# Softmax sums of sixteen heads in one tile: one reciprocal and two shuffles in place of two reciprocals

## The chip, the cores and the metric

The kernel runs on one core of a Trainium2 chip. The metric is the device time of one execution in microseconds (us), taken as the median of several runs. The core's engines are TensorE (PE in the profile, its weight loads PEld), VectorE (DVE), ScalarE (ACT), GpSimd (POOL) and SyncE (SP, which issues transfers). PSUM is the memory that TensorE writes, in banks of 512 f32 columns by 128 partitions.

## The reference

Two layers over x of shape (2, 1024, 256) and a context of shape (2, 64, 192), cut to what matters here:

```python
# layer 0: cross attention with 16 heads of 16 columns, 64 keys, then a small MLP
q = (x @ Wq + bq).reshape(B, N, 16, 16)
k = (y @ Wk + bk).reshape(B, M, 16, 16)
v = (y @ Wv + bv).reshape(B, M, 16, 16)
attn = softmax(einsum('bnhd,bmhd->bhnm', q, k) * scale)
out = einsum('bhnm,bmhd->bnhd', attn, v).reshape(B, N, 256)
x = x + (relu(out @ W1 + b1) @ W2 + b2)      # q is computed from layernorm(x)
# then: a gated LoRA FFN with 8 experts (wi, wo, lora_A, lora_B, gate_w), top 2,
# layer 1: single-head cross attention, and a linear layer with pooled columns
```

The change touches the division by the sums of the first softmax.

## The kernel before, in words

The 2048 rows are worked in 8 blocks of T = 256 rows. Three stages are in flight at once: `body(a, f, c, h)` runs, on each engine, the first attention and MLP of block a, the FFN of block f = a - 1, the last attention of block c = a - 2, and the queries of block h = a + 1. Below, "block a" means the pass whose first attention is block a. Passes 0 and 1 have no c and take the `else` branches; passes 2 to 7 take the `if C_` branches. After the passes come `drain` and `end`. Each engine has its own program written out by hand, in a fixed order; engines meet only at semaphores, and an engine that waits holds everything behind it in its own order.

Products that need more than fp32r precision are made as three passes over high and low halves (`passes`, L341, and `three`, L332): high by high, low by high, high by low. The high half comes from ACT, the low half from POOL or DVE.

Attention of a block on PE: `a_scores(a, d)` (L411) makes scores of four heads for d = 0 to 3 into `psS`; ACT's `exps` (L896) turns them into `ex`, where a chunk c of 8 holds a pair of heads, 64 keys each, on 128 partitions. `a_attend(a, m)` (m = 0, 1) then takes four chunks. For each it multiplies the values (L425) into 32 partitions of bank `P_(m)`, columns 0 to 255, and a matrix of ones, `ones_pair`, into columns 256 to 511 of the same rows (L426), so each head's sum stands on the 16 partitions of that head. After each m it signals `pv`.

DVE's `attended(a, m)` waits for `pv`, takes the reciprocal of the 128x256 sums (L1193, to `rec`), waits for it, and multiplies the values by it into `o32` (L1195). ACT's `attended` makes the high half `oa_h` (L901), POOL's `attended_low` the low half `oa_l` (L1562). PE's `a_hidden(a, 0)` (L341, `psS<-oa_h,w_h`) waits for both high halves, and before its third pass for both low halves.

Around it, in the order of each engine:

- PE in pass 0: scores 2, two filler products, attend 0, scores 3, attend 1, `values1` (L608), transposes (L356), fillers, `a_hidden(0, 0)`. In pass 1: attend 0, second products of FFN parts 0 and 1 (L490), scores 3, `f_base` 2 (L332), attend 1, `f_first` 2, `f_base` 3, `f_second` 2, `f_first` 3, `a_hidden(1, 0)`, transposes that wait for `gw`, `a_hidden(1, 1)`, `a_queries` (whose third pass waits for `xta_l`). In passes 2 to 7: attend 0, attend 1, `f_second` 1, `c_transpose` (L547), `f_base` 2, `f_first` 2, `c_attend` (L557, waits for `et_l`), `f_base` 3 (waits for the sum of FFN part 1), and so on to `a_hidden`.
- DVE in passes 2 to 7: `hidden_sum` 0 (L1252), `attended` 0, `hidden_sum` 1, `weights_low` (L1282, makes `et_l`), `attended` 1, then the sums and residuals of block c. In passes 0 and 1: `hidden_sum` 0 and 1 (pass 1 only), `attended` 0, `attended` 1, and in pass 1 then `gw` (L1411), `hidden_sum` 2, `vv_l` (L1417), `xta_l` (L1163).
- ACT in pass 0 after its two `attended`: `xta_h` (L863), then the high halves of the weights w2 and wi (L965, `w_h` and `wi_h`), then `hidden` (L907) and what follows it. `first_relu` 2 is L927.

The ones come with the load `kept` of 424 columns (32 + 256 + 8 + 128), issued third on the SP queue.

Of the kernel before, what the change touches and what calls it, by code (L numbers as in the profile page):

```python
# [11 lines left out]
P = 128  # L12
BATCH, SEQ, D = 2, 1024, 256
KEYS, DC = 64, 192
# [36 lines left out]


FIRST = [("ident", P), ("cols", 20), ("kmask", 8), ("pmask", 2)]
KEPT = [("ones_pair", PW), ("b2row", D), ("gbrow", EXPERTS), ("eid", P)]

VROWS = [("vmask", D), ("bvrow0", D)]
PASSING = [("bvrow1", D), ("wq1t", KC * D)]
# [3 lines left out]
def build(nc, io):  # L61
# [8 lines left out]
    def r3(t, a, lo=0, hi=None, rows=P):  # L70

        v = t[0:rows, lo:hi] if hi is not None else t[0:rows, lo:]
        return v.rearrange("p (a n) -> p a n", a=a)
# [40 lines left out]
    def views(t, parts):  # L114
        out, at = {}, 0
        for n, width in parts:
            out[n] = t[:, at:at + width]
            at += width
        return out
# [1 line left out]
    first = sb("first", [P, sum(n for _, n in FIRST)])  # L121
    kept = sb("kept", [P, sum(n for _, n in KEPT)])
    ident, cols, kmask, pmask = (views(first, FIRST)[n] for n, _ in FIRST)
    ones_pair, b2row, gbrow, eid = (views(kept, KEPT)[n] for n, _ in KEPT)
    nbi = sb("nbi", [P, NFF])
    crow = sb("crow", [P, D])
    mhalf = sb("mhalf", [P, NT])
# [44 lines left out]
    EX = r3(ex, PAIRS)  # L172
    rec, o32 = sb("rec", [P, KC * T]), sb("o32", [P, KC * T])
    REC, O32 = r3(rec, KC), r3(o32, KC)
    lnst = {j: (sb(f"st{j}", [P, NT * 6]), sb(f"mv{j}", [P, NT * 2]), sb(f"ve{j}", [P, NT]), sb(f"nm{j}", [P, NT]),
                sb(f"rs{j}", [P, NT]), sb(f"nmr{j}", [P, NT])) for j in (1, 2, 3, 4)}
    lg, srt, srtd, srte = (sb(n, [P, NT * EXPERTS]) for n in ("lg", "srt", "srtd", "srte"))
# [47 lines left out]
    with block:  # L225
# [97 lines left out]
        def _(pe):  # L323
# [91 lines left out]
            def a_attend(b, m):  # L415

                if m == 0 and b % BPB == 0:
                    pe.wait_ge(S("v0_ready"), b // BPB + 1)
                    pe.wait_ge(S("ld_kept"), 16)
                at = b // BPB * D  # L420
                for d in (2 * m, 2 * m + 1):
                    pe.wait_ge(S("ex"), b * DPAIRS + d + 1)
                    for c in (2 * d, 2 * d + 1):
                        rows = slice(PW * (c % GPC), PW * (c % GPC) + PW)
                        mm(P_(m)[rows, 0:T], v0[:, at + c * PW:at + (c + 1) * PW], EX[:, c, :], start=True, stop=True)  # L425
                        last = mm(P_(m)[rows, T:2 * T], ones_pair, EX[:, c, :], start=True, stop=True)  # L426
                last.then_inc(S("pv"), 1)

            def a_hidden(b, u):
                if u == 0:  # L430
# [421 lines left out]
        def _(act):  # L852
# [46 lines left out]
            def attended(b, m):  # L899
                act.wait_ge(S("o32"), b * KC + m + 1)  # L900
                A(OA[0][:, m, :], O32[:, m, :], ACT.Identity).then_inc(S("oh"), 1)  # L901
# [20 lines left out]
            def first_relu(b, u, bank=None):  # L922
                bank = I_(u % 2) if bank is None else bank
                act.wait_ge(S("first_ps"), b * NDF + u + 1)
                for k in range(2):
                    f = 2 * u + k
                    last = A(R1[:, f, :], bank[:, k * T:(k + 1) * T], ACT.Relu, bias=cols[:, BI + f:BI + f + 1])  # L927
                last.then_inc(S("r1"), 1)
# [82 lines left out]
            def body(a, f, c, h):  # L1011
                A_, F_, C_, H_ = (v is not None for v in (a, f, c, h))
                if A_:
                    exps(a, 0)
                if F_:
                    lora_high(f)
                if A_:
                    exps(a, 1)
                if f == 0:
                    act.wait_ge(S("v1t_ps"), 1)  # L1020
                    A(v1t[:, :], T_(0), ACT.Identity).then_inc(S("v1t"), 1)
                    act.wait_ge(S("v1"), 1)
                    A(VV[0][:, 0:2 * BATCH:2, :], r3(v1, BATCH), ACT.Identity).then_inc(S("vv_h"), 1)
                if C_:
                    linear(c)
                    first_relu(f, 0)
                    exps(a, 2)
                    exps(a, 3)
                    weights_exp(c)
                    first_relu(f, 1)  # L1030
                    if H_ and h < TURNED:
                        normalise(1, h, XIN)
                    elif H_:
                        across_high(h)
                    sum_high(f, 0)
                    weights_high(c)
                    attended(a, 0)
                    sum_high(f, 1)
                    first_relu(f, 2)
                else:  # L1040
                    if F_:
                        first_relu(f, 0)
                        first_relu(f, 1)
                    exps(a, 2)
                    if F_:
                        sum_high(f, 0)
                    exps(a, 3)
                    normalise(1, h, XIN)
                    if F_:
                        sum_high(f, 1)  # L1050
                    attended(a, 0)
                    if F_:
                        first_relu(f, 2)
                if A_:
                    attended(a, 1)
                if F_:
                    first_relu(f, 3)
                if f == 0:
                    act.wait_ge(S("gw"), 1)
                    A(gw_h[:, :], gw[:, :], ACT.Identity).then_inc(S("gw_h"), 1)  # L1060
                if a == 0:
                    high(1, h, XTA, T_(1))
                    high_weights("w2")
                    high_weights("wi")
                if f == 0:
                    high(1, h, XTA, T_(1))
                if A_:
                    hidden(a, 0)
                    hidden_high(a, 0)
                    hidden(a, 1)  # L1070
                if C_:
                    hidden_high(a, 1)
                if H_:
                    queries(h)
                if A_ and not C_:
                    hidden_high(a, 1)
                if a == TURNED - 2:
                    centred_high()
                if f == 0:
                    act.wait_ge(S("vw_ps"), 1)  # L1080
                    A(VV[0][:, 1:2 * BATCH:2, :], T_(0).rearrange("p (b n) -> p b n", b=BATCH), ACT.Identity).then_inc(
                        S("vv_h"), 1)
                if a == 0:
                    high_weights("ga")
                    high_weights("lb")
                    high_weights("wo")
                if F_:
                    sum_high(f, 2)
                    sum_high(f, 3)
                if A_:  # L1090
                    normalise(2, a, XMID)
                    high(2, a, XTF, T_(1))
                if a == 0:
                    act.wait_ge(S("g_ps"), 1)
                    for b in range(BATCH):
                        A(GWR[:, :, b * (KEYS + D):b * (KEYS + D) + KEYS],
                          T_(0)[:, 0:KC * P].rearrange("p (c b k) -> p c b k", c=KC, b=BATCH)[:, :, b, :],
                          ACT.Identity).then_inc(S("g_in"), 1)
                    act.wait_ge(S("gb_ps"), 1)
                    A(gb[:, :], I_(0)[:, 0:P], ACT.Identity).then_inc(S("gb"), 1)  # L1100
                if H_:
                    maxima(h)
                if F_:
                    high(3, f, XTC, T_(0))
                if A_:
                    sorted_exps(a)
                if C_:
                    store(c)
# [29 lines left out]
        def _(dve):  # L1138
# [48 lines left out]
            def row_max(b, t, ps=psS):  # L1187
                dve.wait_ge(S("row_sc"), b * NT + t + 1)
                V.reduce_max(MX[:, t, :], ps[:, :].rearrange("p (h k) -> p h k", h=HEADS), AX.X).then_inc(S("mx"), 1)

            def attended(b, m):
                dve.wait_ge(S("pv"), b * KC + m + 1)
                V.reciprocal(REC[:, m, :], P_(m)[:, T:2 * T]).then_inc(S("rec"), 1)  # L1193
                dve.wait_ge(S("rec"), b * KC + m + 1)
                V.tensor_tensor(O32[:, m, :], P_(m)[:, 0:T], REC[:, m, :], MULT).then_inc(S("o32"), 1)  # L1195

            def first_residual(b):
# [187 lines left out]
            def body(a, f, c, h):  # L1385
# [7 lines left out]
                    norm_stats(1, h, XIN)  # L1393
                if C_:
                    hidden_sum(f, 0)
                    attended(a, 0)
                    hidden_sum(f, 1)
                    weights_low(c)
                    attended(a, 1)
                    weights_sums(c)  # L1400
                    third_residual(c)
                    scaled_linear(c)
                else:
                    if F_:
                        hidden_sum(f, 0)
                        hidden_sum(f, 1)
                    attended(a, 0)
                    attended(a, 1)
                if f == 0:
# [359 lines left out]
```

## Time and profile before

| | |
|---|---|
| median of 3 runs | 321.26 us (321.03 to 321.32) |
| span of the profiled execution | 319.5 us, first to last instruction |
| time of the profiled execution itself | not given apart; the median less the span is 1.8 us |
| mean granted TensorE clock | 0.989 of full speed |
| PE busy | 307.6 us, 96% |
| DVE busy | 233.1 us, 73% |
| ACT busy | 170.4 us, 53% |
| POOL busy | 161.4 us, 51% |

Busy shares are averages over stages with different limits. The span starts with loads and the first block, when weights are still being split into halves; it ends with a drain in which less and less work is left. The time of a change is read from the place where it lengthens or shortens what is waited for last.

### The profile page before, as it was taken

The page shows a single profiled execution, that of the slowest core. Times are in us where ns is not written, and L with a number is a line of the kernel's source. Part 1 is how long each engine was busy: PE and PEld are TensorE (multiplying, and loading weights), DVE is VectorE, ACT ScalarE, POOL GpSimd, SP SyncE. Part 2 cuts the span into 40 slices and gives each one's busy share as a digit, 9 for nine tenths or more (in the row PEclk, how much of TensorE's full clock was granted, in tenths as well). Part 3 has the DMA queues.
Part 4 walks back from the last instruction along what each step waited for, and adds up shares of the span by engine and source line. Part 5 has one row for each costly group of instructions (what it writes and reads, how often), then busy time and mean ns, then how long its engine had stood idle before and what let it go on. Part 6 is the DMA issues. An engine that isn't in the chain of part 4 may idle for free.

```text
span 319.5 us, 6462 instructions
## 1 busy us (share of the span) xinstructions
PE 307.6 (96%) x2469; PEld 281.6 (88%) x2469; DVE 233.1 (73%) x648; ACT 170.4 (53%) x346; POOL 161.4 (51%) x155
## 2 busy tenths in 40 slices
PE   7889999999999999999999999999999999999973
PEld 5658897899989998999989998999899989999961
DVE  4766775967986977867896689678868779456665
ACT  3447755682575358455647457635753574434520
POOL 2574683695055704672286407560557143703561
PEclk9999999999999999999999999999999999999995
DMA  7479730013101240114020421033022200000000
GB/s 254 141 240 383 195 84 2 0 31 78 60 1 19 69 131 0 18 41 125 35 19 17 92 92 16 3 91 109 1 18 64 69 4 0 2 25 10 0 33 33
DMA packets 16861, 20.80 MB, mean 65 GB/s; under 512 B 3104, under 2 KB 12832, under 8 KB 16576
## 3 DMA queue, kind: packets, MB, share of 16 engines
q1 hardware_dynamic: 14800, 16.97, 20.0%
q10 hardware_dynamic: 2032, 3.44, 3.1%
q8 instruction: 19, 0.31, 0.4%
q14 instruction: 10, 0.08, 0.1%
HBM read 11.48 MB, written 2.63 MB: 44 GB/s over the span
## 4 chain that ended last, share of the span: by engine, by line
PE 82%; DVE 6%; ACT 5%; DMA 2%; POOL 2%; SPq 2%; issue 1%; DVEq 0%; POOLq 0%
PE psI L332 14%; PE psI L490 14%; PE psP L341 11%; PE psI L341 10%; PE psS L341 6%; PE psT L332 4%; PE psP L425 3%; PE psS L411 2%; PE psP L426 2%; PE psT L557 2%; PE psT L356 2%; PE psS L388 2%; PE psP L654 1%; DMA xin<-in_x 1%; PE psS L332 1%; PE psP L466 1%
## 5 line engine op out<-in xcount | busy, mean ns | idle before, releaser
L1554 POOL TENSOR_TENSOR rs<-ve,mhalf 128x2 f32<-128x2 f32 x30 | 22.5, 749 | 96.8 <-DVE ve L1159 96.8
L1573 POOL TENSOR_TENSOR hid_l<-r,hid_h 128x512 fp32r<-128x512 f32 x32 | 42.2, 1330 | 16.8 <-ACT hid_h L932 16.6
L927 ACT ACTIVATE r<-psI,first 128x256 f32<-128x256 f32 x60 | 25.2, 477 | 19.8 <-PE psI L490 19.8
L490 PE MATMUL psI<-at_h,lb_h 128*128 128x256 f32 x120 | 35.1, 292 | 0.0
L1252 DVE SCALAR_TENSOR_TENSOR r<-psI,nbi,r 128x256 f32<-128x256 f32 x60 | 26.1, 477 | 11.4 <-PE psI L490 11.4
L490 PE MATMUL psI<-at_l,lb_h 128*128 128x256 f32 x120 | 33.9, 282 | 0.0
L490 PE MATMUL psI<-at_h,lb_l 128*128 128x256 f32 x120 | 33.7, 281 | 0.0
L1567 POOL TENSOR_TENSOR hs_l<-hs,hs_h 128x512 fp32r<-128x512 f32 x16 | 20.9, 1307 | 21.8 <-ACT hs_h L912 21.0
L1193 DVE RECIPROCAL rec<-psP 128x256 f32<-128x256 f32 x16 | 28.0, 1753 | 2.7 <-PE psP L426 2.7
L858 ACT ACTIVATE xn<-xmid,nmr,rs 128x256 f32<-128x256 f32 x16 | 8.8, 594 | 38.0 <-POOL nmr L1558 38.0
L896 ACT ACTIVATE ex<-psS 128x512 f32<-128x512 f32 x32 | 18.3, 599 | 19.0 <-PE psS L411 18.9
L490 PEld LDWEIGHTS psI<-at_h,lb_h 128*128 128x128 f32 x120 | 22.6, 188 | 3.9 <-issue 3.5
L332 PE MATMUL psI<-xtf_h,wi_h 128*128 128x256 f32 x120 | 25.9, 297 | 0.0
L332 PE MATMUL psI<-xtf_h,wi_l 128*128 128x256 f32 x120 | 24.1, 282 | 0.0
L332 PE MATMUL psI<-xtf_l,wi_h 128*128 128x256 f32 x120 | 23.9, 280 | 0.0
L932 ACT ACTIVATE hid_h<-r 128x512 fp32r<-128x512 f32 x32 | 19.6, 630 | 6.0 <-DVE r L1252 6.0
L490 PEld LDWEIGHTS psI<-at_h,lb_l 128*128 128x128 f32 x120 | 22.6, 189 | 0.0
L490 PEld LDWEIGHTS psI<-at_l,lb_h 128*128 128x128 f32 x120 | 22.6, 188 | 0.0
L332 PEld LDWEIGHTS psI<-xtf_h,wi_h 128*128 128x128 f32 x120 | 18.2, 189 | 2.4 <-issue 2.2
L890 ACT ACTIVATE stack<-psP 16x1024 fp32r<-16x1024 f32 x16 | 16.2, 1015 | 4.4 <-PE psP L397 4.1
L332 PEld LDWEIGHTS psI<-xtf_l,wi_h 128*128 128x128 f32 x120 | 18.4, 188 | 0.0
L332 PEld LDWEIGHTS psI<-xtf_h,wi_l 128*128 128x128 f32 x120 | 18.4, 188 | 0.0
(274 smaller groups left out, 868.2 us busy)
## 6 DMA issues: line engine op xcount, KB each, us to landing
stack<-qu_h SPq DMA_DIRECT2D x60, 64.0 KB, 2.0
xin<-in_x SPq DMA_DIRECT2D x8, 256.0 KB, 2.9
stack<-qu_l SPq DMA_DIRECT2D x30, 64.0 KB, 2.0
out<-x ACTq DMA_DIRECT2D x7, 256.0 KB, 2.0
xn<-in_xt SPq DMA_DIRECT2D x5, 256.0 KB, 3.0
raw_wi<-in_wi SPq DMA_DIRECT2D x1, 1024.0 KB, 7.9
raw_wo<-in_wo SPq DMA_DIRECT2D x1, 1024.0 KB, 10.3
kv<-in_kv SPq DMA_DIRECT2D x2, 384.0 KB, 5.2
```

Source lines behind the costliest of these rows:

```text
L332: last = mm(out, lhs(a, c), rhs(b, c), start=start and q == 0 and k == 0, stop=stop and q == 2 and k == n - 1, **kw)
L341: last = mm(out, lhs(a, c), rhs(b, c), start=start and (a, b) == pairs[0] and i == 0 and k == 0, stop=stop and k == len(chunks) - 1, skip_ ...
L490: last = mm(bank[:, k * T:(k + 1) * T], (WH, WL)[x]["lb"][:, 0, f * P:(f + 1) * P], AT[y][:, which, :], start=False, stop=q == 2, skip_gro ...
L890: A(QS[3 * PW:SROWS, :, t * P:(t + 1) * P], P_(1)[t * MXW:t * MXW + HEADS, 0:P].unsqueeze(1).broadcast_to([HEADS, PAIRS, P]), ACT.Identity ...
L896: A(EX[:, 2 * d:2 * d + 2, :], S_(d % 2).rearrange("p (k n) -> p k n", k=2), ACT.Exp, scale=SCALE).then_inc(S("ex"), 1)
L927: last = A(R1[:, f, :], bank[:, k * T:(k + 1) * T], ACT.Relu, bias=cols[:, BI + f:BI + f + 1])
L932: A(HH[:, 2 * u:2 * u + 2, :], R1[:, 2 * u:2 * u + 2, :], ACT.Identity).then_inc(S("hidh"), 1)
L1193: V.reciprocal(REC[:, m, :], P_(m)[:, T:2 * T]).then_inc(S("rec"), 1)
L1252: last = V.scalar_tensor_tensor(out=R1[:, f, :], in0=bank[:, k * T:(k + 1) * T], scalar=nbi[:, f:f + 1], in1=R1[:, f, :], op0=MAX, op1=ADD)
L1554: G_.tensor_tensor(rs[:, :], ve[:, :], mhalf[:, :], ALU.pow).then_inc(S(f"ln{j}_rs"), 1)
L1567: G_.tensor_tensor(HS[1][:, two, :], HS32[:, two, :], as32(HS[0][:, two, :]), ALU.subtract).then_inc(S("hsl"), 1)
L1573: G_.tensor_tensor(HL[:, two, :], R1[:, two, :], as32(HH[:, two, :]), ALU.subtract).then_inc(S("hidl"), 1)
```

## The change

The ones become `ones_lanes`, two 128x32 matrices. Matrix m sends a pair's two sums to 8 partitions each of its 32: the first head to partitions 8m to 8m + 7, the second to 16 + 8m to 16 + 8m + 7, and zeros to the others. The products with both matrices are accumulated in one tile, columns 256 to 511 of bank `P_(1)`, which after both halves of `a_attend` holds the sums of all 16 heads on 8 partitions each. `pv` is signalled once a block instead of twice. DVE takes one reciprocal of that tile (`inverses`), and `attended(a, m)` spreads it over the 16 partitions of each head with a `stream_shuffle` within groups of 32 partitions, then multiplies as before. In passes 2 to 7 `inverses` stands where `attended` 0 stood, and `attended` 0 moves behind `weights_low`. On ACT, `attended` 0 moves behind `first_relu` 2. The number of matrix products stays the same. `kept` grows by 32 columns.

```diff
-KEPT = [("ones_pair", PW), ("b2row", D), ("gbrow", EXPERTS), ("eid", P)]
+LANES = 8
+KEPT = [("ones_lanes", KC * PW), ("b2row", D), ("gbrow", EXPERTS), ("eid", P)]
...
+    INV = REC[:, 1, :]
...
-                        mm(P_(m)[rows, 0:T], v0[:, at + c * PW:at + (c + 1) * PW], EX[:, c, :], start=True, stop=True)
-                        last = mm(P_(m)[rows, T:2 * T], ones_pair, EX[:, c, :], start=True, stop=True)
-                last.then_inc(S("pv"), 1)
+                        mm(P_(m)[rows, 0:T], v0[:, at + c * PW:at + (c + 1) * PW], EX[:, c, :], start=m == 0, stop=True,
+                           skip_group_check=True)
+                        last = mm(P_(1)[rows, T:2 * T], ones_lanes[:, m * PW:(m + 1) * PW], EX[:, c, :], start=m == 0,
+                                  stop=m == 1, skip_group_check=True)
+                if m == 1:
+                    last.then_inc(S("pv"), 1)
...
(ACT, both branches of body)
-                    attended(a, 0)
                     sum_high(f, 1)
                     first_relu(f, 2)
+                    attended(a, 0)
...
(DVE)
+            def inverses(b):
+                dve.wait_ge(S("pv"), b + 1)
+                V.reciprocal(INV, P_(1)[:, T:2 * T]).then_inc(S("rec"), 1)
+
             def attended(b, m):
-                dve.wait_ge(S("pv"), b * KC + m + 1)
-                V.reciprocal(REC[:, m, :], P_(m)[:, T:2 * T]).then_inc(S("rec"), 1)
-                dve.wait_ge(S("rec"), b * KC + m + 1)
+                if m == 0:
+                    dve.wait_ge(S("rec"), b * 3 + 1)
+                even, odd = LANES * m, HD + LANES * m
+                V.stream_shuffle(REC[:, m, :], INV, [even] * HD + [odd] * HD).then_inc(S("rec"), 1)
+                dve.wait_ge(S("rec"), b * 3 + 2 + m)
                 V.tensor_tensor(O32[:, m, :], P_(m)[:, 0:T], REC[:, m, :], MULT).then_inc(S("o32"), 1)
...
                     hidden_sum(f, 0)
-                    attended(a, 0)
+                    inverses(a)
                     hidden_sum(f, 1)
                     weights_low(c)
+                    attended(a, 0)
                     attended(a, 1)
...
                         hidden_sum(f, 1)
+                    inverses(a)
                     attended(a, 0)
                     attended(a, 1)
```

## Rows read from the trace of the kernel before

**Rows 1.** Part 1 of the page: busy time, share of the span, instructions.
```profile
PE 307.6 (96%) x2469; PEld 281.6 (88%) x2469; DVE 233.1 (73%) x648; ACT 170.4 (53%) x346; POOL 161.4 (51%) x155
```

**Rows 2.** Busy time by stretch: start:end, length, engines, granted clock, DMA share, GB/s.
```profile
10.00:20.00 10.00, 8.79 (x45) 6.66 (x44) 8.99 (x15) 4.03 (x6) 6.94 (x4) 1.00 0.55 150
29.00:37.00 8.00, 7.84 (x61) 7.20 (x60) 4.32 (x5) 7.97 (x13) 5.96 (x5) 1.00 0.93 312
82.00:116.00 34.00, 34.00 (x293) 32.21 (x292) 26.27 (x78) 19.27 (x40) 17.12 (x17) 1.00 0.19 42
...
310.00:314.00 4.00, 2.69 (x9) 1.61 (x8) 2.56 (x11) 1.40 (x5) 0.22 (x1) 0.81 0.00 0
```

**Rows 3.** Waits of PE from 60 to 290 us: total, times, longest.
```profile
PE psT L356 <- ACT xn L858: 0.3, 1, 0.3
PE psP L341 <- POOL hs_l L1567: 0.2, 1, 0.2
```

**Rows 4.** Chain that ended last, in pass 0: start, us, what.
```profile
25.78 1.69 DVE rec L1193
...
27.95 0.42 ACT oa_h L901
...
28.86 0.95 ACT w_h L965
29.80 1.80 ACT wi_h L965
...
35.07 1.30 POOL hs_l L1567
...
36.41 1.22 PE psP L341 x8
```

**Rows 5.** Groups of DVE instructions: busy, mean ns of one, idle before.
```profile
L1193 DVE RECIPROCAL rec<-psP 128x256 f32<-128x256 f32 x16 | 28.0, 1753 | 2.7 <-PE psP L426 2.7
...
L1163 DVE TENSOR_TENSOR xtf_l<-psT,xtf_h 128x512 fp32r<-128x512 f32 x8 | 5.5, 692 | 12.9 <-ACT xtf_h L863 12.9
...
L1219 DVE MATCH_VALUE_LOAD idx<-srt,lg 128x8 f32 x16 | 1.3, 79 | 0.0
...
L1536 DVE COPY wqm<-psI 128x256 f32<-128x256 f32 x1 | 0.4, 425 | 0.1
...
L1509 DVE MEMSET zeros<- 128x256 f32 x1 | 0.3, 272 | 0.0
```

**Rows 6.** Timeline of pass 0: start, us, instruction, idle before.
```profile
25.36 0.42 DVE L1195 TENSOR_TENSOR o<-psP,rec 128x256 f32<-128x256 f32 x1
25.70 1.76 DVE L1193 RECIPROCAL rec<-psP 128x256 f32<-128x256 f32 x1
...
27.49 0.42 DVE L1195 TENSOR_TENSOR o<-psP,rec 128x256 f32<-128x256 f32 x1
```

**Rows 7.** Timeline of pass 1.
```profile
61.49 0.42 ACT L901 ACTIVATE oa_h<-o 128x256 fp32r<-128x256 f32 x1 [0.56 <-DVE o L1195]
...
62.74 0.64 PE L341 MATMUL psS<-oa_h,w_h 128*128 128x256 f32 x4
...
65.55 0.68 DVE L1163 TENSOR_TENSOR xta_l<-psT,xta_h 128x512 fp32r<-128x512 f32 x1
...
66.98 0.64 PE L341 MATMUL psP<-xta_l,wq_h 128*128 128x256 f32 x4
```

**Rows 8.** Timeline of pass 2.
```profile
90.54 0.66 PE L425 MATMUL psP<-ex,v 128*32 128x256 f32 x8
...
91.86 0.65 PE L426 MATMUL psP<-ex,kept 128*32 128x256 f32 x8
...
93.86 0.86 DVE L1252 SCALAR_TENSOR_TENSOR r<-psI,nbi,r 128x256 f32<-128x256 f32 x2
...
94.64 0.28 DVE L1282 TENSOR_TENSOR et_l<-psT,et_h 128x128 fp32r<-128x128 f32 x1
...
95.59 0.50 PE L557 MATMUL psT<-vv_h,et_h 64*128 64x512 f32 x2
```

More of the change, by code:

```diff
@@ L123, in build @@
     ident, cols, kmask, pmask = (views(first, FIRST)[n] for n, _ in FIRST)
-    ones_pair, b2row, gbrow, eid = (views(kept, KEPT)[n] for n, _ in KEPT)
+    ones_lanes, b2row, gbrow, eid = (views(kept, KEPT)[n] for n, _ in KEPT)
     nbi = sb("nbi", [P, NFF])
@@ L1395, in body @@
                     hidden_sum(f, 0)
-                    attended(a, 0)
+                    inverses(a)
                     hidden_sum(f, 1)
                     weights_low(c)
+                    attended(a, 0)
                     attended(a, 1)
@@ L1731 @@
         "vmask": (p[:, None] // KEYS == (c[None, :] // HD) % 2).astype(np.float32),
-        "ones_pair": (p[:, None] // KEYS == np.arange(PW)[None, :] // HD).astype(np.float32),
+        "ones_lanes": (2 * (p[:, None] // KEYS) + np.arange(KC * PW)[None, :] // PW
+                       == np.arange(KC * PW)[None, :] % PW // LANES).astype(np.float32),
         "eid": np.broadcast_to((p // RANK).astype(np.float32)[None, :], (P, P)),
```

## The prediction

> **What bounds the kernel now.** I read four views in this order. The page's busy times come first: PE works 96% of the span [rows 1], so time taken from DVE is worth something only where PE, or whoever holds PE up, waits for DVE. The second view is the busy time by stretch, which says where PE is not full. In a whole pass of the steady part it is busy 34.00 of 34.00 us, while DVE works 26.27 of them [rows 2]. The third is the list of PE's waits: from 60 to 290 us they come to 0.5 us, none of them for DVE [rows 3]. So the six passes 2 to 7 have no idle PE time that a lighter DVE could win back. The fourth is the chain that ended last. It is PE nearly everywhere from 36.41 us on, but in pass 0 it runs through the very instructions that are changed: the reciprocal, the multiply, `oa_h` on ACT, then without a gap `xta_h`, `w_h`, `wi_h`, `hidden` and what follows, POOL's `hs_l`, and PE at 36.41 [rows 4]. PE itself is busy 7.84 of 8 us there [rows 2], partly with fillers, and yet the chain is ACT's: whatever makes `oa_h` of m = 1 later moves the end of the kernel one for one. The question is thus not what DVE saves, but how long the road is from the last attention product to the second `oa_h`.
>
> **What the change removes and adds on DVE.** Gone in each block is one reciprocal of 1.753 us [rows 5]. Two shuffles of 128x256 are added. The trace has no shuffle. The nearest rows are the copy of 128x256, 0.425 us, and below it the memset of the same size, 0.272 us, which reads nothing; above, the 128x512 subtraction, 0.692 us, twice the columns [rows 5]. A shuffle is a copy through a permutation, with as many columns as the copy, so I take 0.42 us, and keep 0.27 and 0.69 for the range. The Trainium skill (VectorE: DVE Perf Modes, "The perf-mode tier table (the rule you actually need)") gives a shuffle about 2400 ns at 2048 columns. My estimate from that page is 0.30 us for 256, which would make the sum below 0.5 us smaller; no row here shows a shuffle.
>
> A shuffle also needs its permutation. The nearest row for handing an engine such a small table is `MATCH_VALUE_LOAD`, 0.079 us ahead of each index search [rows 5]. I take 0.08 us ahead of each shuffle, with 0 and 0.16 as bounds. The Trainium skill (Vector Engine (DVE) Microarchitecture Reference, section 3.8) has the selection written by an instruction of its own before the shuffle, and gives no time for it.
>
> DVE's work falls by 1.753 - 2 x (0.42 + 0.08) = 0.75 us a block, 6 us in all. Off the path, this is worth nothing.
>
> **The road in pass 0.** Before, the first reciprocal and multiply run while PE still does attend 1, and the second reciprocal starts at 25.70; its multiply starts at 27.49 and ends at 27.91 [rows 6]. An instruction that waits for its forerunner thus starts 0.03 us after that one's end, and one that needs nothing of it starts 0.34 us after the start of a multiply (25.36 to 25.70). Now DVE must wait for both halves of the attention. They end at about 25.7, which is where the second reciprocal already stood, so the start does not move. After it stand the reciprocal as before, and then, new ahead of the last multiply: table 0.08, shuffle 0.42 + 0.03, the first multiply 0.34 to the next issue, table 0.08, shuffle 0.42 + 0.03. Sum 1.40 us: the second `o32` is ready at 29.3 instead of 27.9. Nothing on ACT, behind it in order, has a gap before `hs_h` ends, and POOL's `hs_l` follows [rows 4], so PE's third pass of `a_out` moves from 36.41 to 37.8. From there PE is the chain. **+1.40 us.** By the bounds: 0.27 + 0.03 + 0.34 + 0.27 + 0.03 = 0.94 at the least, 0.16 + 0.72 + 0.34 + 0.16 + 0.72 = 2.10 at the most.
>
> **The road in pass 1.** Here too attend 1 is over by the time the second reciprocal started, and the same pieces are put ahead of the last multiply. The second `oa_h` ran from 61.49 to 61.91; 1.40 later it ends at 63.31. PE's `a_hidden` began at 62.74 [rows 7] and must wait 0.57 us. Queued on DVE behind `attended` are `gw`, `hidden_sum` 2, `vv_l` and `xta_l`, with little idle time between them, so `xta_l` comes at 65.55 + 1.40 = 66.95 and ends at 67.63. PE's third pass of the queries stood at 66.98 [rows 7], by now 67.55, and waits another 0.08. I see no further late comer. **+0.65 us.** With the cheap shuffle `oa_h` ends at 62.85, +0.11, and `xta_l` again 0.08 late, so +0.19; with the dear one, 2.10 later, at 64.01, +1.27, and `xta_l` ends at 68.33, 0.08 after 68.25, so +1.35.
>
> **Passes 2 to 7.** Here DVE has `inverses` where it had `attended` 0. The attention products end at 91.86 + 0.65 = 92.51 in pass 2, so I let the reciprocal start at 92.6, against 91.73 before [rows 8]. It ends at 94.36, `hidden_sum` 1 takes 0.86, `weights_low` 0.28: `et_l` is there at about 95.4, against 94.92 before. PE asks for it at 95.59 [rows 8]. A margin of about 0.2 us is left, and the shuffles do not stand ahead of it, since `attended` 0 was moved behind. Both shuffles and multiplies then take 2 x (0.08 + 0.45) + 0.34 + 0.42, and the second `o32` ends near 97.2, where `a_hidden` starts near 99.4: hidden. `hidden_sum` 1 (at 95.2, for `f_base` 3 after 96.5) is hidden too. On ACT the moved `attended` 0 costs nothing: `a_hidden` waits for the second half anyway. **0**, with 0 to 0.1 a pass as bounds, so 0.6 at the most.
>
> **The rest.** PE's products are as many and of the same shapes, only their bank and the accumulate flag differ: 0. `kept` grows from 212 to 228 KB; the load of x stands ahead of it on the queue: 0, at most 0.1. Drain and end have no such attention.
>
> **Sum.** 1.40 + 0.65 + 0 = +2.05 us on the profiled span of 319.5, so 321.55. The median is 1.76 above that span, which gives **323.3 us**. By the bounds 0.94 + 0.19 = +1.13 (322.4) and 2.10 + 1.35 + 0.6 + 0.1 = +4.15 (325.4).
>
> **Rivals.**
>
> *The path gets no longer where it counts (same).* In pass 0 ACT's two large copies need weights that are just landing, and the DMA share there is 0.93 [rows 2]. If it were the landing and not ACT's order that released `wi_h` at 29.80, and with a lag of its own above 1 us, most of the 1.40 would vanish. Against it: `w_h` and `wi_h` follow each other with no gap [rows 4]. What is left is pass 1, +0.65 or less: 321.3 to 321.9. Chance 0.08.
>
> *The attention gets shorter (faster).* The sums of m = 0 now go to another bank than the values. If this lets the products of a block overlap better, each of eight blocks wins. The products of pass 2 run from 90.54 to 92.51, 2.0 us [rows 8]; saving 0.3 of it is 2.4 us in all, against 2.05 lost: 320.9. It decides from 0.26 us a block. Against it: nothing in the trace has a product waiting for a bank. Chance 0.04.
>
> *The margin in passes 2 to 7 is gone (slower still).* If the tile of both halves is signalled 0.4 us later than I think, or accumulating costs PE something, `c_attend` waits 0.2 us each time: 6 x 0.2 = +1.2, so 324.5. For it speaks how thin 0.2 us is; against it, that its terms are all rows. Chance 0.12.
>
> *The clock falls.* PE idles some 1.4 us more between 29 and 38. At 310 to 314, with 2.69 of 4 us busy, the granted clock was 0.81, that is partly at 1.2 GHz; at 10 to 20, with 8.79 of 10 busy, it stayed at 2.4 GHz [rows 2], and the new stretch is more like the second. If half of 8 us of work ran at half speed, 4 us more: 327. Chance 0.03.
>
> *The forecast*, +1 to +3.5 us from the two roads of passes 0 and 1: chance 0.73; its own range is 322.3 to 324.8.
>
> **How the numbers follow.** A change within 0.2%, 0.64 us, is about what a measurement of this kernel cannot tell from none; it is 320.6 to 321.9. Slower: forecast 0.73, thin margin 0.12, clock 0.03: 0.88. Same: 0.08. Faster: 0.04. The range of 8 in 10 goes from 321.9, just at the foot of the forecast, to 324.8, which takes in the thin margin at my price.
>
> **What would show it.** In the changed profile: one 128x256 reciprocal a block, eight in all; shuffles near 0.42 us, with or without a small load ahead; from the reciprocal's start to the end of the second multiply in pass 0 some 3.6 us instead of 2.2; a wait of PE for `oa_h` in passes 0 and 1, near 0.9 and 0.6 us, and a longer one for `hs_l` or ACT before 38 us; no wait of PE for `et_l` later; a whole steady pass still 34.0 us. I am wrong if the steady pass has another length, if ACT's `wi_h` starts no later than before, or if the shuffle costs far from 0.42.

## The result and the profile after

The changed kernel took 321.98 us (median of 12 runs, 321.58 to 322.42) against 321.07 us (12 runs, 320.19 to 321.63) for the kernel before. The ratio is 1.0035, 95% interval 1.0022 to 1.0047: slower by 0.35%. That is 0.9 us by the medians and 1.1 us by the ratio. I had forecast slower, 323.3 us, with a range from 321.9 to 324.8. The direction is right and the time lies at the very foot of the range: of the +2.05 us of my sum about half came, which is less than the least that my bounds for the terms allow, +1.13.

The page of the changed kernel, part 1 as in [rows 1], shows what the change was to do for DVE:

```profile
PE 308.4 (96%) x2469; PEld 282.6 (88%) x2469; DVE 225.7 (70%) x672; ACT 169.6 (53%) x346; POOL 160.3 (50%) x155
```

DVE works 7.4 us less. Its groups answer to [rows 5], busy, mean ns of one, idle before:

```profile
L1198 DVE RECIPROCAL rec<-psP 128x256 f32<-128x256 f32 x8 | 14.1, 1757 | 12.2 <-PE psP L429 12.2
L1204 DVE STREAM_SHUFFLE rec<-rec 128x256 f32<-128x256 f32 x16 | 7.1, 443 | 0.0
L1204 DVE LOAD_MASK_SELECT rec<-rec x16 | 0.2, 13 | 0.1
```

The shuffle costs 0.443 us, hardly more than the copy I took it for, and the load of its permutation 0.013 us, not 0.08. The reciprocals fall from 28.0 to 14.1 us, the shuffles and their loads put back 7.3: 6.6 of the 7.4 us come from the change itself, and 0.64 of the rest from another instruction, `wq_l`, which is met below. The reciprocal now waits 12.2 us in all for PE, against 2.7.

The busy time by stretch, as in [rows 2]: in a whole steady pass PE is as full as before, with about 1 us less work on DVE.

```profile
29.00:38.00 9.00, 8.06 (x59) 7.28 (x60) 4.43 (x5) 8.97 (x15) 6.88 (x6) 1.00 0.91 284
82.00:116.00 34.00, 34.00 (x293) 32.24 (x293) 25.23 (x81) 19.10 (x41) 17.07 (x17) 1.00 0.16 36
```

From 29 to 38 us PE is idle 0.94 us, and the granted clock stays at 1.00, the higher level. The chain that ended last, in pass 0, answers to [rows 4]: start, us, what.

```profile
25.40 1.77 DVE rec L1198
27.17 0.03 issue
27.20 0.45 DVE rec L1204 x2
27.65 0.02 issue
27.67 0.36 DVE o L1206
28.04 0.44 DVE rec L1204
28.48 0.02 issue
28.50 0.43 DVE o L1206
28.93 0.02 issue
28.95 0.42 ACT oa_h L906
...
29.86 0.95 ACT w_h L970
30.80 1.81 ACT wi_h L970
...
36.06 1.30 POOL hs_l L1580
37.36 0.04 issue
37.40 1.22 PE psP L343 x8
```

The road is the one I drew. From the reciprocal's start to the end of the last multiply it is 3.53 us, where before it was 2.21 from 25.70 to 27.91 [rows 6]. ACT's `wi_h` moved from 29.80 to 30.80, and PE's third pass of `a_out` (the second product of the block's MLP, L343 with `hs_l`) from 36.41 to 37.40. Both are this 1.3 less the 0.3 by which this run reached the reciprocal earlier. `wi_h` moved with the road and still follows `w_h` without a gap, so it was ACT's order that released it, and not the landing of its weights.

In the steady passes the margin ahead of `c_attend` stayed open. `et_l` of pass 2 ends at 96.31, 0.37 us ahead of the first product of `c_attend`, where I had left 0.2; in passes 3 to 7 it is the same 0.37, and PE's list of waits behind 80 us has none for `et_l`.

```profile
96.03 0.28 DVE L1293 TENSOR_TENSOR et_l<-psT,et_h 128x128 fp32r<-128x128 f32 x1
...
96.68 0.51 PE L562 MATMUL psT<-vv_h,et_h 64*128 64x512 f32 x2
```

**A ruler.** Five of the profiled kernels (those named "after" in the table) have the same program up to the first attention product, and yet it comes between 21.23 and 22.27 us in them. That start is jitter of 1 us, so I compare stretches between fixed points: the first attention product of pass 0, of pass 1, of pass 2, the last `c_attend`, and the end of the span. Here are the first two kernels' first points (PE's timeline, start and us); before:

```profile
22.38 0.66 PE L425 MATMUL psP<-ex,v 128*32 128x256 f32 x8
53.46 0.66 PE L425 MATMUL psP<-ex,v 128*32 128x256 f32 x8
```

and after:

```profile
22.07 0.66 PE L427 MATMUL psP<-ex,v 128*32 128x256 f32 x8
54.46 0.66 PE L427 MATMUL psP<-ex,v 128*32 128x256 f32 x8
91.60 0.66 PE L427 MATMUL psP<-ex,v 128*32 128x256 f32 x8
```

Each kernel's stretches, all in us from its profiled execution, with the experiments that follow (the short names are explained there):

| kernel | start | pass 0 | pass 1 | passes 2 to last `c_attend` | rest | span |
|---|---|---|---|---|---|---|
| before | 22.38 | 31.08 | 37.08 | 207.57 | 21.4 | 319.5 |
| after | 22.07 | 32.39 | 37.14 | 207.78 | 21.1 | 320.5 |
| pass 0 old | 21.44 | 31.10 | 37.17 | 207.77 | 21.4 | 318.9 |
| passes 0, 1 old | 21.92 | 31.10 | 37.02 | 207.87 | 21.1 | 319.0 |
| before, late wq | 22.28 | 31.06 | 36.89 | 207.73 | 21.0 | 319.0 |
| after, late wq | 22.27 | 32.37 | 37.62 | 207.80 | 21.3 | 321.4 |
| after, no shuffle | 21.41 | 31.39 | 36.69 | 207.84 | 21.1 | 318.4 |
| after, more shuffles | 21.23 | 32.37 | 37.15 | 208.10 | 21.5 | 320.3 |
| before, wq in gap | 22.10 | 31.10 | 36.43 | 207.55 | 21.1 | 318.3 |
| after, wq in gap | 21.73 | 32.35 | 37.16 | 207.83 | 21.1 | 320.2 |
| passes 0, 1 old, wq in gap | 21.88 | 31.08 | 36.45 | 207.82 | 21.1 | 318.3 |
| before, kept padded | 21.32 | 31.07 | 37.04 | 207.69 | 21.1 | 318.2 |

Between the first two rows: start -0.31, pass 0 +1.31, pass 1 +0.06, the steady part +0.21, the rest -0.27, in all +1.0. Pass 0 is as forecast (+1.40). Pass 1, where I had put +0.65, grew by 0.06 only.

**Where the 0.65 us of pass 1 went.** PE does lose time there, in both places I named. From its timeline in the changed kernel, pass 1, beside [rows 7]:

```profile
64.26 0.74 PE L343 MATMUL psS<-oa_h,w_h 128*128 128x256 f32 x4 [0.38 <-ACT oa_h L906]
...
67.85 0.68 DVE L1168 TENSOR_TENSOR xta_l<-psT,xta_h 128x512 fp32r<-128x512 f32 x1
...
68.61 0.70 PE L343 MATMUL psP<-xta_l,wq_h 128*128 128x256 f32 x4
```

`a_hidden` moved from 62.74 to 64.26, and the third pass of the queries from 66.98 to 68.61, +1.63: 1.0 from pass 0, the rest lost here. Counted from the first attention product of pass 1, instruction by instruction in the two traces, PE is late by 0.52 us at the first product of `a_hidden`, by 0.62 from its second on, by 0.70 behind the third pass of the queries (whose first product starts 0.08 us after `xta_l` ends; the trace names no wait there), and by 0.73 before it comes to the transposes of `xn`. I had forecast 0.57 and 0.08. The waits for `oa_h` itself are shorter than I wrote: 0.5 us in pass 0 and 0.38 in pass 1, for 0.9 and 0.6.

But over the transposes of `xn`, the normalised rows, the 0.73 shrink to 0.12. Here are two instructions that run there beside PE in the kernel before: POOL's `hid_l`, the low half of the FFN's hidden values, and DVE's `wq_l`, the low half of the centred query weights, which is made once, in pass 1, and which only the queries of pass 2 need:

```profile
71.19 2.99 POOL L1573 TENSOR_TENSOR hid_l<-r,hid_h 128x512 fp32r<-128x512 f32 x2
71.67 1.35 DVE L1177 TENSOR_TENSOR wq_l<-qs,wq_h 128x512 fp32r<-128x512 f32 x1
...
77.84 0.93 PE L356 MATMUL psT<-first,xn 128*128 128x128 f32 x4
```

and in the changed kernel:

```profile
73.37 0.71 DVE L1182 TENSOR_TENSOR wq_l<-qs,wq_h 128x512 fp32r<-128x512 f32 x1
73.49 2.98 POOL L1586 TENSOR_TENSOR hid_l<-r,hid_h 128x512 fp32r<-128x512 f32 x2
...
79.30 0.60 PE L358 MATMUL psT<-first,xn 128*128 128x128 f32 x4
```

The same DVE instruction takes 1.35 us before and 0.71 us after. Before, it started 0.48 us after POOL's first `hid_l`, with 0.81 us of that one to go; after, 0.12 us ahead of it, with 0.16 us to go of the POOL instruction before, `hs_l`. It stands on DVE's chain to `xn`, for which PE waits before the transposes: the group of four took 0.93 us before, with waits inside, and 0.60 after. So my theory became: the roads of passes 0 and 1 cost what I forecast, and the delay in pass 1 happens to move `wq_l` out from behind POOL's `hid_l`, which pays most of pass 1's part back.

### The profile page after: what moved, and what is told of

Read it like the earlier page. It is cut to its first block, busy times and chain, and to the rows that moved or that the text cites. A ratio compares the mean times of both kernels' runs of the same rounds, so it can differ in the third digit from the quotient of the medians.

```text
span 320.5 us, 6486 instructions
## 1 busy us (share of the span) xinstructions
PE 308.4 (96%) x2469; PEld 282.6 (88%) x2469; DVE 225.7 (70%) x672; ACT 169.6 (53%) x346; POOL 160.3 (50%) x155
## 4 chain that ended last, share of the span: by engine, by line
PE 85%; DVE 5%; ACT 4%; SPq 2%; DMA 1%; POOL 1%; issue 1%; DVEq 0%
PE psI L334 13%; PE psI L495 13%; PE psP L343 12%; PE psI L343 11%; PE psS L343 6%; PE psT L334 4%; PE psP L427 3%; PE psS L413 3%; PE psP L429 2%; PE psS L390 2%; PE psT L562 2%; PE psT L358 1%; PE psP L659 1%; PE psS L334 1%; PE psP L683 1%; PE psP L471 1%
## 5 line engine op out<-in xcount | busy, mean ns | idle before, releaser
L932 ACT ACTIVATE r<-psI,first 128x256 f32<-128x256 f32 x60 | 25.2, 476 | 18.7 <-PE psI L495 18.6
L1580 POOL TENSOR_TENSOR hs_l<-hs,hs_h 128x512 fp32r<-128x512 f32 x16 | 20.8, 1303 | 21.3 <-ACT hs_h L917 21.1
L1198 DVE RECIPROCAL rec<-psP 128x256 f32<-128x256 f32 x8 | 14.1, 1757 | 12.2 <-PE psP L429 12.2
L1194 DVE TENSOR_REDUCE mx<-psS 128x16 f32<-128x1024 f32 x15 | 18.2, 1216 | 0.3 <-PE psS L390 0.3
```

The costliest lines, as they stand in the source:

```text
L1580: G_.tensor_tensor(HS[1][:, two, :], HS32[:, two, :], as32(HS[0][:, two, :]), ALU.subtract).then_inc(S("hsl"), 1)
```

## The experiments

All were run beside the kernel before on the same chip, in three sets; the kernel before took 321.11, 321.06 and 320.94 us in them. The changed kernel was not run again beside them, so where an experiment is compared with it, this goes by the ratios to the kernel before, or by the stretches in the table.

### Undoing the change pass by pass

The new form needs all passes' counts adjusted; the core of the edit, `OLD` being the passes in the old form. In the first kernel it is (0,), in the second (0, 1):

```diff
+                        if b in OLD:
+                            mm(P_(m)[rows, 0:T], v0[:, at + c * PW:at + (c + 1) * PW], EX[:, c, :], start=True, stop=True)
+                            last = mm(P_(m)[rows, T:2 * T], ones_pair, EX[:, c, :], start=True, stop=True)
+                            continue
...
+                if b in OLD:
+                    dve.wait_ge(S("pv"), PV0(b) + m + 1)
+                    V.reciprocal(REC[:, m, :], P_(m)[:, T:2 * T]).then_inc(S("rec"), 1)
...
+            V.tensor_copy(ones_pair, vmask[:, 0:PW]).then_inc(S("ones"), 1)
```

> The changed kernel with pass 0 alone back in the old form (two signals, two reciprocals, no shuffle, ones_pair copied from vmask), passes 1 to 7 in the new. Theory A (the road of pass 0 costs 1.3 us; pass 1 costs 0.6 to 0.7 us on its road but gets 0.6 us back because wq_l on DVE no longer stands behind POOL's hid_l): the first attention product of pass 1 comes 36.7 to 36.8 us after that of pass 0 less 1.3, so 35.7 instead of 37.0, and the median is 0.0 to 0.3 us under the kernel before. Rival B (the cost is spread over the passes, a wait in each): under 0.4 us of the 0.9 us is won back.

> Passes 0 and 1 back in the old form, passes 2 to 7 in the new. Theory A: the same as the kernel before within 0.3 us, since each steady pass costs 0.03 us or less, and about the same as the kernel with pass 0 alone put back, since the cost and the gain of pass 1 cancel. My prediction as it stood (pass 1 costs a full 0.65 us): 0.65 us under the kernel with pass 0 alone put back. Rival B: most of the 0.9 us remains.

Measured: pass 0 alone put back, 321.07 us, ratio to the kernel before 1.0005 (0.9994 to 1.0015); passes 0 and 1 put back, 321.12 us, ratio 1.0000 (0.9983 to 1.0018). In the table pass 0 falls from 32.39 to 31.10 in both (I had written 37.0 and 35.7 for this stretch, which was a slip: the numbers are 32.4 and 31.1; the 1.3 us between them came). The whole loss is gone with pass 0, so rival B, a cost spread over the passes, falls. And putting back pass 1 too changes little, 37.17 and 37.02 for that pass and nothing in the medians, against the 0.65 us of my prediction. In the first, where pass 1 is new, `wq_l` took 0.70 us; in the second, where it is old, 1.36 us.

### Moving wq_l: a first place

```diff
-                if a == TURNED - 2:
-                    centred_low()
...
                 if A_:
                     low(2, a, XTF, T_(1))
+                if a == TURNED - 2:
+                    centred_low()
```

> The kernel before, with one DVE instruction moved: centred_low (wq_l, 128x512, in pass 1) goes from behind queries_low to behind xtf_l of the same pass; it is needed only by the queries of pass 2. Theory A (wq_l stands 1.35 us on DVE's chain to xn of pass 1, of which 0.64 us is waiting for POOL, and PE waits 0.6 us for xn there): 0.5 to 0.6 us faster than the kernel before. Rival C (PE's wait for xn has another cause, and the overlap with POOL is of no weight): no change.

> The changed kernel with the same instruction moved. Theory A: the gain is there already, so 0 to 0.1 us faster than the changed kernel, and 1.4 to 1.8 us slower than the kernel before with wq_l moved: that is the cost of the change once the overlap is out of both. Rival C: no change against the changed kernel, and 0.9 to 1.1 us slower than the kernel before with wq_l moved.

Measured: 321.07 us, ratio 1.0001 (0.9981 to 1.0021), for the kernel before with `wq_l` moved; 322.92 us, ratio 1.0056 (1.0044 to 1.0069), for the changed one. Taken one by one, both are misses: no gain on the first, where 0.5 to 0.6 us was expected, and on the second a ratio of 1.0056 against the changed kernel's 1.0035, some 0.7 us lost where 0 to 0.1 was to be gained. The trace shows why. In the first kernel the products of `hid_l` that follow the transposes began 24.45 us after the first product of pass 1, against 25.07 before: the 0.6 us are won there. Then they are lost again, because `wq_l` now stands ahead of `second_residual`, for which PE waits in `c_turn` (the transposes of the block's result `x`; timeline of the kernel before with `wq_l` late):

```profile
71.08 2.52 POOL L1573 TENSOR_TENSOR hid_l<-r,hid_h 128x512 fp32r<-128x512 f32 x2
...
79.31 0.68 DVE L1177 TENSOR_TENSOR wq_l<-qs,wq_h 128x512 fp32r<-128x512 f32 x1
...
81.52 0.63 PE L528 MATMUL psT<-first,x 128*128 128x128 f32 x4 [0.31 <-DVE x L1260]
```

With `wq_l` away, POOL's pair of `hid_l` takes 2.52 us instead of 2.99. My place was badly chosen, but it is the same in both kernels, and so the pair does tell the theories apart. The medians are 1.85 us apart, a little above the 1.4 to 1.8 of theory A and far from the 0.9 to 1.1 of rival C, and pass 1 is 36.89 without the change and 37.62 with it, +0.73 where the unmoved pair shows +0.06.

### Moving wq_l: into DVE's gap

```diff
-                if a == TURNED - 2:
-                    centred_low()
...
                 if H_:
                     row_max(h, 1)
+                if a == TURNED - 2:
+                    centred_low()
```

> The kernel before with wq_l moved to behind the second row_max of pass 1, where DVE idles about 2 us ahead of xtf_l; the earlier place behind xtf_l held up second_residual and c_turn. Theory A: pass 1 falls from 37.08 to 36.4 to 36.5 us (first attention product to first attention product), and the kernel is 0.6 us faster than before. Rival C: 37.1 and no change.

> The changed kernel with the same instruction moved to the same gap. Theory A: pass 1 stays at 37.1 (PE is full there), pass 0 at 32.4; the kernel is within 0.1 us of the changed kernel and 1.9 to 2.1 us slower than the kernel before with wq_l in the gap, 1.3 of it in pass 0 and 0.65 to 0.75 in pass 1: that is the sum of my prediction, 2.05. Rival C (wq_l does not matter): 0.9 to 1.1 us slower.

Measured: 320.41 us for the kernel before with `wq_l` in the gap, ratio 0.9987 (0.9970 to 1.0005), and 322.28 us for the changed kernel with it there, ratio 1.0041 (1.0027 to 1.0056). The medians are 1.87 us apart, against the 1.9 to 2.1 expected. In the table: pass 0 31.10 and 32.35, +1.25; pass 1 36.43 and 37.16, +0.73; together 1.98. Rival C, that `wq_l` is of no weight, falls. Against the changed kernel the second has a ratio of 1.0041 for 1.0035, 0.2 us more where I had allowed 0.1; the intervals overlap. The instruction itself, in the kernel before with `wq_l` in the gap, has again met a POOL instruction that started ahead of it, and takes as long as ever, only where nobody waits:

```profile
76.19 1.28 POOL L1590 TENSOR_TENSOR xr<-xin,kept 128x512 f32<-128x512 f32 x1
...
76.65 1.36 DVE L1177 TENSOR_TENSOR wq_l<-qs,wq_h 128x512 fp32r<-128x512 f32 x1
...
77.31 0.60 PE L356 MATMUL psT<-first,xn 128*128 128x128 f32 x4
```

The transposes take 0.60 us, without the waits. The gain of the whole, 0.65 us in the medians, is just not clear of the measurement on its own; the stretch of pass 1, 37.08 and 36.43, is.

### Without the shuffles

```diff
-                if m == 0:
-                    dve.wait_ge(S("rec"), b * 3 + 1)
-                even, odd = LANES * m, HD + LANES * m
-                V.stream_shuffle(REC[:, m, :], INV, [even] * HD + [odd] * HD).then_inc(S("rec"), 1)
-                dve.wait_ge(S("rec"), b * 3 + 2 + m)
-                V.tensor_tensor(O32[:, m, :], P_(m)[:, 0:T], REC[:, m, :], MULT).then_inc(S("o32"), 1)
+                if m == 0:
+                    dve.wait_ge(S("rec"), b + 1)
+                V.tensor_tensor(O32[:, m, :], P_(m)[:, 0:T], INV, MULT).then_inc(S("o32"), 1)
```

> The changed kernel without its shuffles: attended multiplies by the reciprocals as they stand in the tile, so the spreading of the sums over the heads' rows is left out. Theory A (the cost is the length of the road from the last attention product to the second o32, and two thirds of it are the shuffles): from the first attention product of pass 0 to that of pass 1 31.4 us, against 31.08 before and 32.39 after; no wait of PE for oa_h in pass 1, so pass 1 falls back to the 37.1 of the kernel before, wq_l again beside POOL's hid_l; in all 0.9 to 1.0 us under the changed kernel. Rival (the cost is that both halves must be waited for): pass 0 stays above 32 us.

This kernel leaves out the spreading of the sums over the heads' rows, so only its time is read. Measured: 320.88 us, ratio 1.0002 (0.9988 to 1.0017) against the changed kernel's 1.0035, 1.1 us less. Pass 0 is 31.39: the shuffles are 1.0 of the 1.3 us, and waiting for both halves costs the 0.3 of one multiply, as the pieces of the road say. Pass 1 came out at 36.69, not 37.1. Here `wq_l` took a third length, 1.00 us, 0.35 less than in the kernel before, and pass 1 is 0.39 us shorter. It started at 71.00, in the last half microsecond of POOL's `hs_l`:

```profile
68.90 2.57 POOL L1577 TENSOR_TENSOR hs_l<-hs,hs_h 128x512 fp32r<-128x512 f32 x2
...
71.00 1.00 DVE L1182 TENSOR_TENSOR wq_l<-qs,wq_h 128x512 fp32r<-128x512 f32 x1
71.42 2.99 POOL L1583 TENSOR_TENSOR hid_l<-r,hid_h 128x512 fp32r<-128x512 f32 x2
```

The lengths follow one rule. For each trace, this is when `wq_l` ran, and when the single POOL instruction ended that was at work as it started:

| kernel | `wq_l` starts | POOL's instruction ends | `wq_l` ends | length | end behind POOL's |
|---|---|---|---|---|---|
| before | 71.68 | 72.48 (`hid_l`) | 73.03 | 1.35 | 0.55 |
| before, wq in gap | 76.65 | 77.47 (`xr`) | 78.02 | 1.37 | 0.55 |
| after, no shuffle | 71.00 | 71.46 (`hs_l`) | 72.01 | 1.00 | 0.55 |
| after | 73.37 | 73.53 (`hs_l`) | 74.08 | 0.71 | 0.55 |
| pass 0 old | 71.48 | 71.63 (`hs_l`) | 72.18 | 0.70 | 0.55 |
| before, late wq | 79.31 | none at work | 79.99 | 0.68 | |

In all ten traces in which it meets POOL, `wq_l` ends 0.54 to 0.55 us after that instruction, whether 0.15 or 0.82 us of it were left. And the `hid_l` instruction that starts before `wq_l` is done takes 1.74 to 1.76 us, where its like takes 1.28 to 1.32, and ends 1.15 to 1.16 us after `wq_l`. Each of the two is held until the other has ended; had they only slowed each other down, the lag would grow with the time they share. DVE's row maximum, which reads PSUM (`mx<-psS`), ran beside `hid_l` in the changed kernel and took 1.21 us, no more than elsewhere.

### More shuffles in the steady passes

```diff
+                more = 2 if b >= 2 else 0
+                if m == 0:
+                    for k in range(more):
+                        V.stream_shuffle(REC[:, m, :], INV, [even] * HD + [odd] * HD).then_inc(S("rec"), 1)
+                        dve.wait_ge(S("rec"), REC0(b) + 2 + k)
```

> The changed kernel with three shuffles instead of one ahead of the first multiply in passes 2 to 7 only, 0.94 us more on DVE in each. Theory A (the shuffles of the steady passes are hidden, nothing waits for the second o32 there): a steady pass stays at 34.1 us, the median within 0.2 us of the changed kernel. Rival B (the steady passes pay): up to 0.94 us a pass, 5.6 us in all.

Measured: 322.35 us, ratio 1.0045 (1.0030 to 1.0060), against 1.0035 for the changed kernel: 0.3 us more, where I had allowed 0.2, with intervals that overlap widely. The steady part took 208.10 instead of 207.78, 0.3 us for 5.6 us more of DVE's time. The shuffles of the steady passes are hidden, nearly all. This does not test the thin margin that I had given 12 in 100, since the added shuffles stand behind `et_l`; that one held by the 0.37 us read above.

### The steady passes alone in the new form, and the wider load

The first is the kernel with passes 0 and 1 old, plus the move into the gap. The second adds nothing but columns:

```diff
-KEPT = [("ones_pair", PW), ("b2row", D), ("gbrow", EXPERTS), ("eid", P)]
+KEPT = [("ones_pair", PW), ("spare", PW), ("b2row", D), ("gbrow", EXPERTS), ("eid", P)]
```

> Passes 0 and 1 in the old form, passes 2 to 7 in the new, and wq_l in the gap of pass 1. Theory A: pass 0 31.1, pass 1 36.4 as in the kernel before with wq_l in the gap, and 0.2 us more than that kernel over the six later passes, so the new form is worth nothing in the steady passes either: a median of 320.4 to 320.8. Rival (the new form wins in the steady passes, where DVE is 0.8 us a pass lighter, once the first two are out of its way): under 320.2.

> The kernel before with kept at the changed kernel's 456 columns, 32 of them zeros that nobody reads. Theory A (the first attention product came at 22.38 before and 22.07 after, 0.3 us apart, by the loads' jitter alone): no change, within 0.2 us of before. Rival D (the wider load, which lands later, moves POOL's xr against DVE's kd_h at the start and so wins about 0.3 us): 0.2 to 0.4 us faster.

Measured: 320.48 us, ratio 0.9984 (0.9975 to 0.9994), for the first; 320.78 us, ratio 1.0003 (0.9993 to 1.0014), for the second. The first is faster than the kernel before by 0.16%, clear of the noise, but the kernel before with `wq_l` in the gap has 320.41, and the two agree in pass 1, 36.45 and 36.43: the gain is `wq_l`'s. The new form, confined to where it is hidden, shows no gain of its own, and its steady part is 0.27 us longer in the table. The wider load shows no gain either: its profiled start is 21.32 against 22.38, about as far apart as the jitter seen above, and its median is within 0.2 us.

## Why the prediction was right, and where it was wrong

- **What bounds the kernel: right.** DVE's 7.4 us less work bought nothing. A steady pass is 34.1 us whether DVE is busy 26.3 of 34 us [rows 2] or 25.2, or has two shuffles more.
- **The price of a shuffle: right**, 0.44 for 0.42. **Its table:** 0.013 for 0.08, which took 0.13 us off each road, and the dearer shuffles put 0.05 back: 1.32 for 1.40. Of the two rules cited, the estimate from VectorE: DVE Perf Modes in the Trainium skill, 0.30 us, came out low for 256 columns, and the row of the copy was nearer; that the permutation has an instruction of its own, as the other says, is what the trace shows.
- **Pass 0, +1.40: right in mechanism and size, measured +1.25 to +1.31.** Putting pass 0 back removes it, taking the shuffles away removes 1.0 of it.
- **Pass 1, +0.65: the two losses came, the sum did not.** The pass grew by 0.06. With `wq_l` taken out of the way it grows by 0.73, so the two losses were sized well. The step that failed is the one behind them, from "I see no further late comer" to +0.65: I looked for what would come later and not for what would get shorter, and took it that a delay of PE within the pass reaches its end whole. The runs show 0.6 us given back at the transposes of `xn`. The trace of the kernel before had the row: a 128x512 subtraction of 1.354 us (`wq_l`, L1177) among others of 0.69 [rows 5], with POOL's `hid_l` beside it, and PE waiting for `xn` behind it.
- **A rule of the Trainium skill speaks of this**, and I had not weighed it. SBUF — State Buffer, section "Who interferes with whom", has a DVE instruction with two SBUF inputs and a GpSimd instruction that reads SBUF shut each other out: the first to start holds the port, the other waits to its end. The lengths of `wq_l` agree: 0.68 us when POOL is not at work, 0.70 to 0.71 with 0.15 to 0.17 us left of POOL's instruction, 1.00 with 0.46 left, and 1.35 to 1.37 with 0.81 to 0.82 left.
- **Passes 2 to 7, 0 with 0.6 at the most: right.** The stretch is 207.77 to 208.10 us in the kernels with the new form there and 207.55 to 207.73 in those without, so some 0.2 us more. No run shows what it is, and it is at the edge of what the profiles repeat.
- **The range: held by luck.** 321.98 is inside it by 0.08 us. Its foot, 321.9, came from what a measurement can tell from none and not from the costs; both the forecast's own 322.3 and the least sum, 322.4, lie above the measured time, because no bound of mine had a term that gives time back.
- **Rivals.** No gain from the products' other bank: the steady stretch is not shorter. The clock did not fall: granted 1.00 from 29 to 38 us, with PE idle for 0.94. "The path gets no longer where it counts" was right for pass 1 in effect, where I had put it for pass 0 and by another mechanism; in pass 0 `wi_h` moved with the road.

That the overlap with POOL is what moved pass 1 is shown by the pairs with and without it, and by the kernel without shuffles, where a `wq_l` shorter by 0.35 us goes with a pass shorter by 0.39. That each waits for the other's end is shown by the constant 0.55 us. That the thing they wait for is a port was not tried by itself.

## What to carry to other kernels

Work saved on an engine that was 73% busy beside one that was 96% busy was worth nothing here, while what the change cost in length of the first block's dependent chain was paid in full: price the chain in the ramp first. When a change shifts one engine against another, look not only for what comes late but for instructions whose length in the trace is well above that of their likes. They may be collisions, as `wq_l` was, and there a shift of 0.6 us against POOL was enough to remove one. Compare stretches between fixed points of the trace, not whole spans: here that told 0.06 us from 0.73 us under a jitter of 1 us at the start.

## What the runs showed of the hardware

- `STREAM_SHUFFLE` of 128x256 f32 takes 0.443 us and its `LOAD_MASK_SELECT` 0.013 us; the reciprocal of the same size takes 1.757 us.
- The 128x512 subtraction `wq_l`, with both inputs in SBUF, took 0.68 us alone and up to 1.37 us behind a POOL instruction: in ten traces it ended 0.54 to 0.55 us after that instruction, however much of it was left. POOL's pair of `hid_l` took 2.98 to 2.99 us when `wq_l` ran into it (changed kernel, kernel before), 2.52 us when it did not (kernel before with `wq_l` late). Neither record shows a wait; the instruction held up only looks longer.
- PE idled 0.94 us in 9 us of the ramp at an unchanged granted clock of 1.00.
